# Moving one dense pass's transposes behind the key transpose, and one between values and projection, in TensorE's order

## The reference, cut to what matters

```python
x = x + gnn(layernorm(x), adj)                 # (16, 512, 128)
h = layernorm(x)
q = (h @ Wq) * 128 ** -0.5                      # 8 heads of 128
scores, idx = product_key_topk(h)              # 16 rows per token and head, of 16384 per head
k = sum_over_16(softmax(scores) * keys_table[idx])
v = sum_over_16(softmax(scores) * values_table[idx])
out = causal_softmax(q @ k.T) @ v
x = x + concat_heads(out) @ Wo
```

## Time and profile before

| what | us |
|---|---|
| median of 3 runs | 9083.97 |
| the 3 runs | 9080.26, 9083.97, 9106.01 |
| span of the profiled execution, first to last instruction | 9083.0 |
| TensorE busy (matrix products) | 7878.3, 87% |
| TensorE loading weights | 6137.2, 68% |
| VectorE busy | 7108.3, 78% |
| GpSimd busy | 6820.4, 75% |
| ScalarE busy | 4886.8, 54% |
| GpSimd idle before gathers, all reasons | 2245.6 |
| of it "issue": nothing that the profile shows | 2168.4 |

### The profile page before, as it was taken

One profiled execution on the slowest core, in us unless ns is written; L12 is line 12 of the kernel. 1 busy time (PEld: TensorE's weight loads), 2 busy tenths in 40 slices (PEclk: granted clock), 3 DMA queues, 4 the chain that ended last, 5 costly groups with the idle time before them and its releaser, 6 DMA issues.

```text
span 9083.0 us, 179526 instructions
## 1 busy us (share of the span) xinstructions
PE 7878.3 (87%) x51232; PEld 6137.2 (68%) x51232; DVE 7108.3 (78%) x30205; ACT 4886.8 (54%) x14163; POOL 6820.4 (75%) x7177
## 2 busy tenths in 40 slices
PE   5988888888888888888888888898888888889898
PEld 4766667667666766766667666676766766667676
DVE  7787787777878778787787877878778787787875
ACT  3555555555555555555555555464555555555554
POOL 5777777777777777777777777777777777777777
PEclk7999999999999999999999999999999999999998
DMA  4555555555555555555555555555555555555554
GB/s 133 170 171 165 168 168 170 168 167 167 172 165 167 171 166 168 170 167 166 166 172 166 168 169 168 168 171 168 169 166 169 168 166 170 172 162 171 162 179 146
DMA packets 445970, 1516.75 MB, mean 167 GB/s; under 512 B 123760, under 2 KB 141552, under 8 KB 379248
## 3 DMA queue, kind: packets, MB, share of 16 engines
q0 software_dynamic: 344064, 939.98, 33.8%
q1 hardware_dynamic: 100848, 564.37, 17.1%
HBM read 1499.66 MB, written 4.19 MB: 166 GB/s over the span
## 4 chain that ended last, share of the span: by engine, by line
POOL 49%; issue 18%; PE 16%; DVE 15%; ACT 1%; DMA 1%; POOLq 0%; DVEq 0%; SPq 0%; ACTq 0%
POOL got L391 49%; PE dense_ps L523 6%; DVE wide L1214 4%; PE comb_ps L664 3%; DVE hits L1178 2%; DVE chosen L1109 2%; PE wideT_ps L509 2%; DVE onehot L1104 1%; PE front_ps L463 1%; DVE onehot L1097 1%; PE score_ps L499 1%; DMA got<-in_table,rows 1%; DVE lifted L1117 1%; PE score_ps L548 1%; PE front_ps L467 1%
## 5 line engine op out<-in xcount | busy, mean ns | idle before, releaser
L391 POOL DMA_INDIRECT got<-in_table,rows x7168 | 6818.5, 951 | 2245.6 <-issue 2168.4
L523 PE MATMUL dense_ps<-tab,wideT 128*128 128x256 f32 x16384 | 4030.5, 390 | 10.6 <-ACT kv_d L725 9.4
L523 PEld LDWEIGHTS dense_ps<-tab,wideT 128*128 128x128 f32 x16384 | 3053.3, 195 | 669.9 <-issue 265.1
L1214 DVE SCALAR_TENSOR_TENSOR wide<-const_ps,rank,expo 128x128 f32<-128x128 f32 x8192 | 2299.3, 343 | 1357.6 <-PE wideT_ps L509 1039.4
L790 ACT ACTIVATE expo<-sim_d,shift 128x128 f32<-128x128 f32 x8192 | 2598.9, 394 | 128.8 <-DVE wide L1214 127.9
L725 ACT ACTIVATE wideT<-wideT_ps 128x512 f32<-128x512 f32 x2048 | 1212.9, 592 | 676.6 <-PE wideT_ps L509 669.9
L509 PE MATMUL wideT_ps<-ident,wide 128*128 128x128 f32 x8192 | 1255.4, 276 | 265.7 <-ACT wideT L725 243.1
L509 PEld LDWEIGHTS wideT_ps<-ident,wide 128*128 128x128 f32 x8192 | 1023.3, 143 | 534.4 <-issue 286.3
L664 PE MATMUL comb_ps<-got,spread 128*32 128x256 f32 x14336 | 1031.5, 436 | 135.6 <-DMA got<-in_table,rows 107.8
L664 PEld LDWEIGHTS comb_ps<-got,spread 128*32 128x32 f32 x14336 | 469.6, 122 | 587.7 <-issue 245.1
L725 ACT ACTIVATE kv<-comb_ps,wsum 128x256 f32<-128x256 f32 x448 | 210.4, 470 | 909.3 <-PE comb_ps L664 909.1
(11 more groups left out here) (167 smaller groups left out, 7386.0 us busy)
## 6 DMA issues: line engine op xcount, KB each, us to landing
tab<-in_dense SPq DMA_DIRECT2D x512, 1024.0 KB
got<-in_table,rows POOLq DMA_INDIRECT x7168, 2.7
adj_i<-in_adj SPq DMA_DIRECT2D x16, 1024.0 KB
x_in<-in_x SPq DMA_DIRECT2D x16, 256.0 KB, 6.4
out<-fin SPq DMA_DIRECT2D x16, 256.0 KB, 6.0
tab<-in_wqpk_t SPq DMA_DIRECT2D x1, 512.0 KB, 10.5
tab<-in_keys_t SPq DMA_DIRECT2D x1, 512.0 KB, 14.8
wq_sb<-in_wq SPq DMA_DIRECT2D x1, 512.0 KB, 13.5
```

The costliest lines, as they stand in the source:

```text
L391: pool.indirect_dma_start(out=got[got_no(n)][:, g, :], out_offset=None, in_=table, in_offset=bass.IndirectOffsetOnAxis(ap=rows[:, t * GATH ...
L523: mm = pe.matmul(dense_ps[:, v * 2 * D:(v + 1) * 2 * D], wideT[k % 2][:, (2 * u + v) * P:(2 * u + v + 1) * P], tab[(k // CHUNK) % 2][:, (2 ...
L1214: last = dve.scalar_tensor_tensor(wide[k % 2][:, 2 * u + v, :], count_ps[:, v, :], rank1[:, 2 * half + v, key:key + 1], expo[k % 2][:, 2 * ...
```

## The change

Both edits are in TensorE's order alone; the other engines' orders, and the instructions themselves, stay. `passes` is split: `lag(b, k, first)` is its `multiply` of two passes earlier, `turn(b, k)` its transposes. Of the last pass in w[0], `turn` stands behind `key_transpose` (and ahead of the dense head's key transpose), while its `multiply` stays ahead of it. Of the last pass in w[4], `turn` stands between `values` (and `values_dense`) and `project`, while its `multiply` stays ahead of `values`, and of the hit counts (`add_hits`).

```diff
--- before.py
+++ after.py
@@ -527,13 +527,16 @@
                                    skip_group_check=True)
             mm.then_inc(dense_done, 1)
 
+        def lag(b, k, first):
+
+            if k >= 2:
+                multiply(b, k - 2)
+            elif not first:
+                multiply(b - 1, PASSES + k - 2)
+
         def passes(b, k0, count, first):
             for k in range(k0, k0 + count):
-
-                if k >= 2:
-                    multiply(b, k - 2)
-                elif not first:
-                    multiply(b - 1, PASSES + k - 2)
+                lag(b, k, first)
                 turn(b, k)
             return k0 + count
 
@@ -667,7 +670,9 @@
 
                 tile, of = dense_tile(b, n, first, last)
                 c = of * 4 + (tile or 0)
-                k = passes(b, k, w[0], first)
+                if w[0]:
+                    k = passes(b, k, w[0] - 1, first)
+                    lag(b, k, first)
                 if n == 11 and not last:
                     pe.wait_ge(q_copied, b * GH + 4)
                     transpose_xn(b * 2 + 2)
@@ -677,6 +682,9 @@
                 if n == 13 and not last:
                     gnn_msg(b + 1)
                 key_transpose(slot, t)
+                if w[0]:
+                    turn(b, k)
+                    k += 1
                 if tile is not None:
                     if n in LEFT:
                         pe.wait_ge(sim_d_copied, b * 2 + 2)
@@ -701,7 +709,9 @@
                 prob_transpose(slot, t)
                 if tile is not None:
                     prob_transpose_dense(c, tile)
-                k = passes(b, k, w[4], first)
+                if w[4]:
+                    k = passes(b, k, w[4] - 1, first)
+                    lag(b, k, first)
                 for g in HITS[1].get(n, ()):
                     add_hits(b, 1, g, g % 2)
                 for g in () if last else HITS[0].get(n, ()):
```

## The result

| | median of 20 runs | lowest and highest |
|---|---|---|
| before | 9079.6 us | 9075.2 and 9106.0 |
| changed | 9091.8 us | 9082.2 and 9096.2 |

The ratio is 1.0013, 95% interval 1.0007 to 1.0018. The changed kernel is slower by 12 us (6 to 16), within the 0.3% of "no change", and within the range. The predicted 9084.8 was 0.8 us above the before that was shown; the real step is some 12 us.

What follows compares the result with a forecast made beforehand. GpSimd's queue of gathers was taken as the bound from 145 us on; 9083.97 us plus 0.8 for the head, with 0 for the loop and for gather stretching, gave 9084.8 us, range 9069 to 9107.

Steps and rivals of the forecast that it cites:

- GpSimd's gathers are the bound, and the loop lies under them: From 145 us on GpSimd's gather queue, 1.256 us per step, sets the time; the other engines' delays cost 0.
- 5.5 us per batch: TensorE's waits for gathers: how much slower the other engines' loop could run before it set the pace; 0.20 us per slot.
- The deadline of 8.9 us: Tightest found for row numbers: slot 12 of batch 3, written at 1984.64, first used at 1993.52.
- The head, +0.8 us: Slot 0, before 145.40 us: the turn moves by 0.78 us and delays GpSimd undiminished; bounds 0.11 to 1.0.
- The worst sum of 6.9 us per batch: Late w[0] turns in a middle batch, 6 × 0.75 + 22 × 0.11; without the gathers' cover 111 us over the run.
- the loop takes over: Slower rival: late turns delay weigh and lift, row numbers miss their gathers; 9107 or 9331 us; chance 6%.
- I take 0 and allow 12 us either way: Gathers stretched by overlapping VectorE lifts: shifted phase taken as neutral, allowance two fifths of the 29 us excess.
- the 2 ns that I had named as the sign of being wrong: GpSimd's mean gather moving from 951 ns by more than 2 would show the prediction wrong.
- two in five: Share of lifts that would have to change sides, meeting a gather or not, for a 12 us shift.
- The loop is the bound already, and savings count: Faster rival: TensorE's saved waits less 111 us shorten the run to 8974 us; chance 1%.
- the 140.9 + 78.8 us: TensorE's waits over the run for headT (140.9) and keyT (78.8), which the two edits could save.
- the reading by busy shares: Taking the engine of highest occupancy, VectorE 78% before GpSimd 75%, VectorE's delays would count: 9084 + 111 = 9195 us.

Runs made afterwards that it cites:

- experiment 6: Kernel before, with the lift split in two and its constant operand copied to PSUM for six of eight tokens: 9063.0 us, ratio 0.9983 to the kernel before.
- experiment 10: Changed kernel plus three small unused VectorE copies ahead of the lift in slots 3, 15 and 19: 9083.3 us, ratio 1.0006 to the kernel before.
- experiments 6 and 7: Lift split, constant operand in PSUM for six of eight tokens, in the kernel before (9063.0 us) and in the changed one (9058.9 us, ratio 0.9979).
- experiment 3: Second edit alone: last turn of w[4] between values and project, w[0] as in the kernel before: 9083.5 us, ratio 1.0007 to the kernel before.

## Why the prediction was right or wrong, point by point

**GpSimd's gathers are the bound, and the loop lies under them: shown.** No profile with all 16 gathers has a wait of GpSimd above 0.3 us behind the first batch. With 12 gathers the time falls by 89 us to the loop's own; from TensorE's waits I had put its slack at 5.5 us per batch, 88 us. Agreement to 1 us is partly luck, as the four runs scatter by 35 us. The deadline of 8.9 us was the tightest only behind the first batch: in the same profile the row numbers of slot 8 of the first batch come 3.84 us ahead of their gather at 225.8 us.

**The head, +0.8 us: shown in its mechanism up to the lift.** The changed kernel's head, beside the earlier trace rows: combination, key transpose, turn and move on TensorE, weigh and row numbers on VectorE, from the timelines:

```profile
114.55 1.93 PE L667 MATMUL comb_ps<-got,spread 128*32 128x256 f32 x32
...
117.08 0.33 PE L547 MATMUL probT_ps<-ident,kv 128*128 128x128 f32 x1 [0.59 <-ACT kv L738]
...
117.25 0.60 PE L509 MATMUL wideT_ps<-ident,wide 128*128 128x128 f32 x4
...
145.58 1.34 PE L499 MATMUL score_ps<-group_of,lifted 128*128 128x16 f32 x8 [3.45 <-DVE lifted L1130]
...
117.95 1.13 DVE L1227 SCALAR_TENSOR_TENSOR wide<-const_ps,rank,expo 128x128 f32<-128x128 f32 x4 [3.06 <-PE wideT_ps L509]
...
147.06 0.19 DVE L1140 TENSOR_SCALAR rows<-score_ps 128x32 uint32<-128x32 f32 x1 [0.58 <-PE score_ps L499]
```

Weigh starts 3.40 us after the combination (117.95 less 114.55), 2.63 before: 0.77 us for a predicted 0.78. The key transpose waits for kv and the turn starts 0.17 us behind it, where I took 0.11. The move then takes 1.34 us for 1.06, part of it at the low clock, which I had not priced: slot 4's gather comes 33.6 us after the combination for 32.5. Over the ten profiles with 16 gathers the lift ends 30.2 to 30.3 us after the combination starts in the old order of slot 0 and 31.0 in the new, so the 0.7 to 0.8 us hold. By the clock under the move slot 4's first gather comes after 32.5 to 33.4 us in the old order and 33.3 to 33.8 in the new: what a single pair of executions shows there is anything from nothing to 1.3 us.

**The worst sum of 6.9 us per batch, "nothing hidden and no gain counted": far too high**, as a price of the loop. Uncovered, the two edits together don't cost 111 us; the median is 20 us lower. Yet the sum was too low as a count of how much later the turns come. I measured from the start of a pass's multiply to the start of its turn, medians over the middle batches. Where a kv wait stands, the turn is 0.84 us later (0.75 predicted), in five slots and not six; in most others it is 0.11 us later, as predicted. In slots 11, 12 and 13, though, work on the next batch stands between the multiply and the key transpose, and the turn went behind that too: 0.55, 1.84 and 3.68 us later, terms that the prediction doesn't have. With them the delays of a middle batch are some 12 to 13 us. Slot 13 of batch 8 on TensorE, multiply and turn, before (1.84 us apart) and changed (5.51):

```profile
4855.57 1.99 PE L523 MATMUL dense_ps<-tab,wideT 128*128 128x256 f32 x8
...
4857.41 0.60 PE L509 MATMUL wideT_ps<-ident,wide 128*128 128x128 f32 x4
...
4853.94 1.99 PE L523 MATMUL dense_ps<-tab,wideT 128*128 128x256 f32 x8
...
4859.45 0.60 PE L509 MATMUL wideT_ps<-ident,wide 128*128 128x128 f32 x4
```

The rival "the loop takes over" fails: the loop is not slower, though the least margin seen behind the first batch fell below the 8.9 us (5.6 and 2.95 us in two profiles of the changed kernel; 6.0 in the second one of before).

**The step that failed** is the one on the gathers' stretching: "I take 0 and allow 12 us either way". The mechanism stood there, with its rows; the size was wrong: the two orders differ by as much as I had allowed, and what was found behind it is the excess. That the time stayed in the range owes something to luck. The mean gather went only from 951 to 952 ns, within the 2 ns that I had named as the sign of being wrong; one nanosecond of the mean is 7 us of the run. Three things in that passage were off. A lift in the bad stretch costs up to 0.52 us and not 0.32. Twelve microseconds at 0.32 us are 38 lifts, one in six of the 225 and not "two in five". And not all of the excess belongs to lifts: 71 gathers of over 1000 ns in the first profile overlap none, 8 us above the median together; at the start of most of them VectorE was at `hits` (L1178) or at the sums of candidates (L1074). The lifts are not thrown at random between the gathers. TensorE takes up some combinations just when a gather has landed (64 waits in the changed kernel), the later work follows at fixed distances, and so a slot's lift can stand at nearly the same offset batch after batch. That this is what fixes it is argued, not tried; the offsets themselves are seen. An order of work picks these offsets, and this one picked worse ones in most executions:

| profile | gathers busy | lift excess | slot 4's first gather to the last |
|---|---|---|---|
| before, first and second | 6818.5, 6811.4 us | 24.6, 18.2 us | 8920.3, 8913.7 us |
| changed, first and second | 6816.9, 6824.3 | 25.4, 31.2 | 8918.4, 8925.8 |
| first edit alone | 6824.1 | 32.3 | 8925.4 |
| second edit alone | 6818.3 | 25.8 | 8919.7 |
| changed, old slot 0 | 6823.0 | 30.2 | 8924.4 |
| changed, later lifts | 6811.6 | 19.1 | 8913.2 |
| one SBUF input, old and new order | 6796.8, 6792.7 | 0.7, 0.9 | 8900.6, 8894.7 |

The last column follows the excess: less the excess it is 8893.0 to 8895.7 us in nine of the ten profiles, and 8899.9 in experiment 6. Between the second profile of each order it differs by 12.1 us, and the lift excess by 13.0. That this excess is the cause is shown twice: moved away by added work it gives back 8 us (experiment 10), and taken away it leaves nothing of the loss of 12 us: the changed order is then 4 us ahead in the medians (experiments 6 and 7). How much of the 12 us it makes in the median execution is not measured: two profiles of each order scatter by 6 to 7 us among themselves, and both of before are of long executions.

The Trainium skill, "SBUF — State Buffer", section "Who interferes with whom", names the condition, two SBUF inputs against a GpSimd instruction that reads SBUF. The traces agree: where the lift comes first the gather is up to 0.52 us longer, and with the operand in PSUM not at all. Where the gather comes first, the lift is up to 0.08 us longer if the two start within 0.045 us of each other, and shows no price otherwise, at 0.69 us. I had read the rule as neutral on average, and left out that an order fixes the phase.

**"The loop is the bound already, and savings count"** fails: the 140.9 + 78.8 us were saved for the most part and the time rose. So does the reading by busy shares, under which VectorE's delays had made 9195.

**The first profile misled in size.** It took the kernel before at an execution with more stretching than its second profile has (24.6 for 18.2 us) and the changed one at one with less (25.4 for 31.2), so their difference of 1.0 us agreed with my +0.8 by chance. The medians of 20 runs did not.

Open: why the first edit and not the second sets the bad offsets (its largest delays are those of slots 11 to 13; no run tried them alone); whether the new order is really ahead by 4 us with the excess gone (in the two profiles 4.1 us lie in the gathers' busy time, 6796.8 for 6792.7, and 2 us in the gaps that experiment 6 has at 305 and 308 us); why the changed kernel gained 33 us by the copy, 2 to 3 more than the excess of its longest profile; what sets the start of the first gather, 42.5 to 46.2 us.

## What to carry to other kernels

Where one engine issues gathers back to back and waits for nothing, its busy time and the fixed gap behind each gather (0.95 and 0.30 us here) are the kernel, and order on the other engines only matters by what it does to that engine. Ask which instructions of VectorE read two inputs from SBUF while GpSimd issues, and move one operand to PSUM: 15 to 33 us here, for one copy at the start. Before reading a difference of 0.1%, look at more than one profile of each kernel, and at where each profiled execution lies among the runs.

## What was unexpected of the hardware

- Whether a gather is stretched depends on an offset of tenths of a microsecond between it and a VectorE instruction: for a lift at 1.20 us the next gather is 0.51 us longer, for one at 1.21 us not at all. This offset repeats from batch to batch: slot 15's lift stood at 0.95 to 0.98 us in 12 of 16 batches.
- Adding three copies to VectorE in three slots of each batch made the kernel 8 us faster.
- The eight products of a move took 1.06 to 1.89 us in the same place of the program, and both in two profiles of the very same kernel. TensorE was idle for 3.45 us ahead of it each time; at 1.06 us in the kernel before the granted clock between 140 and 150 us was 0.83 of full, at 1.89 us in experiment 3 it was 0.66.
